# One routing per unit in the sixth layer's experts, each made for the batch that comes next

## The reference, cut to what matters

```python
h = _layernorm(x + attn_out, ln1_g, ln1_b)
flat = h.reshape(-1, C)
probs = jax.nn.softmax(flat @ router_w.T + router_b, axis=-1)
_, top_i = jax.lax.top_k(probs, 2)
assign = jnp.max(top_i, axis=-1)
for e in range(E):                                   # E = 8
    he = jax.nn.gelu(flat @ w1[e].T + b1[e], approximate=False)
    oe = he @ w2[e].T + b2[e]
    out = jnp.where((assign == e)[:, None], oe, out)
return _layernorm(h + moe_out, ln2_g, ln2_b)
```

## Time and profile before

| | us |
|---|---|
| median of 3 runs | 970.46 (965.96 to 972.46) |
| the profiled execution's own time | 972.93 |
| its span, first to last instruction | 970.8 |

### The profile page before, as it was taken

The page is one execution under the profiler, slowest core; times in us unless marked ns, Lnnn a source line. Parts: engine busy times, 40 slices in busy tenths (PEclk is TensorE's granted clock), DMA queues, the critical chain, the costliest instruction groups (busy, mean ns, idle before and its releaser), DMA issues.

```text
span 970.8 us, 13156 instructions
## 1 busy us (share of the span) xinstructions
PE 710.3 (73%) x3874; PEld 463.1 (48%) x3874; DVE 574.3 (59%) x1924; ACT 348.2 (36%) x629; POOL 252.2 (26%) x304
## 2 busy tenths in 40 slices
PE   2677662849919775767875666767888778789998
PEld 1233232838919541223464645456655423346665
DVE  6666654415406361686454355697867766878754
ACT  6355420514505222534432322211323365443321
POOL 2240466350160444323305231141012110100000
PEclk9999865859958775968777875797999999999999
DMA  6273022333524133026212110002244111044440
GB/s 166 58 261 96 28 87 66 115 98 112 141 74 135 52 109 94 20 69 193 80 53 90 47 41 1 0 1 74 89 149 152 49 50 50 2 88 98 90 109 12
DMA packets 76527, 80.08 MB, mean 82 GB/s; under 512 B 9420, under 2 KB 63365, under 8 KB 75178
## 3 DMA queue, kind: packets, MB, share of 16 engines
q1 hardware_dynamic: 58922, 62.59, 22.4%
q0 software_dynamic: 5120, 10.50, 3.7%
q10 hardware_dynamic: 12416, 6.16, 2.2%
HBM read 49.99 MB, written 23.12 MB: 75 GB/s over the span
## 4 chain that ended last, share of the span: by engine, by line
PE 45%; DVE 24%; issue 15%; ACT 6%; another core or an unknown queue 3%; SPq 2%; POOL 2%; DMA 1%; ACTq 1%; DVEq 0%
PE psum_all L951 5%; PE psum_all L967 4%; DVE s_nmx L1385 4%; PE psum_all L748 3%; PE psum_all L724 3%; PE psum_all L726 3%; PE psum_all L863 2%; PE psum_all L850 2%; PE psum_all L852 2%; PE psum_all L705 2%; ACT s_hT L2183 2%; PE psum_all L664 2%; PE psum_all L798 2%; DVE s_stats L1269 2%
## 5 line engine op out<-in xcount | busy, mean ns | idle before, releaser
L2183 ACT ACTIVATE s_hT<-psum_all 77x1024 f32<-77x1024 f32 x96 | 95.8, 1017 | 56.8 <-PE psum_all L726 41.6
L2630 POOL TENSOR_SCALAR s_vare<-s_mv 128x4 f32<-128x4 f32 x40 | 11.3, 281 | 392.4 <-DVE s_mv L1272 383.5
L1385 DVE TENSOR_REDUCE s_nmx<-psum_all 128x4 f32<-128x308 f32 x192 | 83.2, 473 | 47.4 <-PE psum_all L705 45.0
L724 PE MATMUL psum_all<-s_t,s_ks 128*77 128x512 bf16 x192 | 83.6, 436 | 10.8 <-ACT s_hT L2183 7.0
L726 PE MATMUL psum_all<-s_t,s_ks 128*77 128x512 bf16 x192 | 82.9, 432 | 0.0
L705 PE MATMUL psum_all<-s_ks,s_t 128*128 128x308 bf16 x192 | 55.8, 334 | 34.6 <-DVE s_nmx L1385 20.2
L748 PE MATMUL psum_all<-s_hT,s_v 77*32 77x512 f32 x384 | 58.8, 687 | 28.5 <-ACT s_hT L2183 26.6
L2540 POOL DMA_INDIRECT s_w<-routed_y,s_cT x64 | 61.5, 960 | 69.5 <-issue 69.5
L967 PE MATMUL psum_all<-s_arena,s_hT 128*128 x376 | 63.2, 306 | 21.5 <-issue 20.6
L2526 POOL DMA_INDIRECT routed_x<-s_x_normed,s_cT x64 | 62.9, 982 | 50.0 <-DVE s_cT L1605 31.7
L967 PEld LDWEIGHTS psum_all<-s_arena,s_hT 128*128 128x128 f32 x376 | 55.7, 208 | 26.9 <-issue 25.6
(11 more groups left out here) (309 smaller groups left out, 1489.5 us busy)
## 6 DMA issues: line engine op xcount, KB each, us to landing
s_t<-q_parts SPq DMA_DIRECT2D x66, 128.0 KB, 2.9
routed_y<-s_hT ACTq DMA_DIRECT2D x22, 256.0 KB
s_ks<-s_att SPq DMA_DIRECT2D x72, 77.0 KB, 2.1
q_parts<-s_qparts SPq DMA_DIRECT2D x11, 384.0 KB
s_arena<-in_w SPq DMA_DIRECT2D x2, 2048.0 KB, 10.5
s_arena<-choices SPq DMA_DIRECT2D x4, 1024.0 KB, 5.8
s_arena<-gates SPq DMA_DIRECT2D x8, 512.0 KB, 8.0
s_w<-gates SPq DMA_DIRECT2D x8, 512.0 KB, 7.8
```

The lines of the kernel that those rows point to most:

```text
L724: pe.matmul(PS[0:SK, k + y, :], KS1[:, h, keys], T1[:, u % QS, h // HPG, :], start=True, stop=False)
L1385: read(job, dve.tensor_reduce(nmx[:, u % 2, i, HPG * g:HPG * g + HPG], PS[:, k, 0:HPG * SK].rearrange("p (h s) -> p h s", h=HPG), AX.X, AL ...
L2183: read(("S", L, b, p), nc.scalar.activation(Eexp[:, (PAIRS * u + p) % ES, :, :], PS[0:SK, k:k + 2, :], ACT.Exp))
```

## The change

The routing of batch 2 moves from unit 0 (steps 4, 5 and 7) to the first steps of unit 1, and that of batch 3 from unit 1 (steps 0, 3 and 6) to the first steps of unit 2. Unit 0 keeps the routing of batch 1. In SP's list `place_k(2)` moves ahead of `spread_choices(2)`. No instruction is added or removed.

```diff
 MHA_PLACES = {
-    0: [((0, 0, 1), "front", 1), ((1, 1, 1), "R", 1), ((3, 3, 4), "CT", 1),
-        ((4, 0, 5), "front", 2), ((5, 5, 5), "R", 2), ((7, 6, 7), "CT", 2)],
-    1: [((0, 0, 1), "front", 3), ((3, 3, 3), "R", 3), ((6, 6, 6), "CT", 3)],
+    0: [((0, 0, 1), "front", 1), ((1, 1, 1), "R", 1), ((3, 3, 4), "CT", 1)],
+    1: [((0, 0, 0), "front", 2), ((1, 1, 1), "R", 2), ((3, 3, 3), "CT", 2)],
+    2: [((0, 0, 0), "front", 3), ((1, 1, 1), "R", 3), ((3, 3, 3), "CT", 3)],
 }
@@
             spread_choices(1)
+            place_k(2)
             spread_choices(2)
-            place_k(2)
             spread_choices(3)
```

## The result

The changed kernel took 986.07 us (median of 4 runs, 981.33 to 990.90) against 971.46 (4 runs, 965.96 to 972.71). The ratio is 1.0159, interval 1.0118 to 1.0201: slower by some 15 us (14.6 between the medians). I had forecast 989.5 within 980 to 994, +19.0. The time lies well inside the range, but 14.6 is near the low end (+14.0) of what my own terms allowed.

What follows compares the result with a forecast made beforehand. It took units 1 to 3 to be bounded by their first choice multiplies, with SP's queue able to make the rows late. Unit 2 starting 9.9 us later and lasting 9.1 longer gave 970.46 + 19.0 = 989.5 us, range 980 to 994.

Steps and rivals of the forecast that it cites:

- Unit 0, -2.2: Layer 5's experts: unit 0 gets 2.2 us shorter without batch 2's routing, bounds 1.5 and 2.6.
- The third key block 12.95 us into unit 1: Unit 1: copy, routing and choice add 3.0 us, so this block ends 12.95 us after the first multiply, before 9.95.
- SP's block, 22.5 us from its start to the landing: SP's queue: issues to store 16.36 us, to spreading 1.64, landing 4.5; batch 2's rows hold unit 2 until then.
- Unit 2, +9.1: Unit 2 lengthens from 20.5 to 29.6 us: 2.2 copy and clock, 1.9 DVE work, 5.0 new wait; range 6.4 to 10.1.
- The wait ahead of the queries: Unit 2: DVE waits 5.0 us because ACT copies batch 3's turned choice ahead of layer 6's queries; 3.6 at full clock.
- The low clock behind the 12 us wait: Start of unit 2: after 11 us of waiting, PE's first second product and hidden product run slow, costing 1.1 us.
- "Cost nothing" for `place_q(8)`: SP's list before unit 3: place_q(8) follows spread_choices(3), its rows landing at 765.2, 4.6 us before PE wants them.
- The sum, +19.0: Whole program: unit 2 starts 9.9 us later and lasts 9.1 longer, together +19.0 us.
- In time after all: Rival: batch 2's rows arrive in time, only unit 2's own costs stay; total +6, 976.5 us; chance 0.07.
- not slower: Rival: the routing fits the gaps and unit 0's 2.2 us becomes a gain; 968.3 us; chance 0.03.
- The wait, but not unit 2's costs: Rival: unit 2 starts 9.9 us late, but the filled pipeline takes up the routing, 0 to 3 us; 982; chance 0.12.
- Worse by place_q(8): Rival: place_q(8) or batch 3's rows also come late, +3 to +5 us on top; 994 us; chance 0.08.

Runs made afterwards that it cites:

- e1: Changed kernel with spread_choices(2) back ahead of place_k(2) in SP's list, routings left in their new places; ratio 1.0054 to the kernel before.
- e4: Changed kernel with only ACT's copy of batch 3's turned choice in unit 2 at step 4 in place of 3; ratio 1.0197 to the kernel before.
- e5: e3 with the queries' store ahead of the store of batch 3's choice and its spreading in SP's list; ratio 1.0052 to the kernel before.
- e6: e5 with ACT's copies behind the Gelus: turned rows at step 1 in units 1 and 2, turned choice at step 4 in unit 1; ratio 1.0022.
- e7: Changed kernel with 12 of place_k(2)'s 24 issues ahead of spread_choices(2) and 12 behind it; ratio 1.0134 to the kernel before.
- e10: Kernel before with only batch 2's routing moved to unit 1, batch 3's kept there at steps 2, 4, 6, ACT's copies behind the Gelus; ratio 1.0042.
- e2: Kernel before with only SP's two items swapped, place_k(2) ahead of spread_choices(2), routings in their old places; ratio 1.0127.
- e3: e1 with ACT's copy of batch 3's turned choice in unit 2 at step 4 in place of 3, behind the queries; ratio 1.0065 to the kernel before.

## Why the prediction was right, point by point

- **Unit 0, -2.2:** -2.4 (38.3 to 35.9). In e1, e4, e5, e6, e7 and e10 too.
- **The third key block 12.95 us into unit 1:** 12.85 (698.09 to 710.94). The copy ahead of a Gelu holds DVE up by 0.9 us there (1.26 of idle time in place of the 0.33 of the earlier trace rows); I had 1.1, and e6 shows it by taking it away.
- **SP's block, 22.5 us from its start to the landing:** 21.4 (710.94 to 732.35). I took the 16.36 of the earlier trace rows for issues up to the store; it was 15.13, my lower bound of the earlier trace rows. Store to spreading 1.67, landing 4.5 as taken. The 1.2 us are one issue. The block's 24 issues, before and after (shortest, median and longest in ns):

```profile
L2667 SPq DMA_DIRECT2D s_ks<-s_att x24: 524/591/1766, 713.9 to 729.5; - x24
L2667 SPq DMA_DIRECT2D s_ks<-s_att x24: 524/591/592, 710.9 to 725.4; - x24
```

Before, one of the 24 held SP for 1.77 us; after, none took more than 0.59. The other runs have a longest one of 0.59 (e4) to 1.75 (e2), and the whole block 15.1 to 16.6; what holds one issue up is open. Unit 1 +10.9 in place of the +12.0 that follows from my steps. e2 shows the block at work alone, e7 that it is proportional to the issues.
- **Unit 2, +9.1:** +9.65. Its parts: the multiply of expert 2 stands 6.5 us into the unit in place of 3.9, +2.6 (I had 2.2). Against e1, which has the copy but no 12 us wait and its third multiply 4.8 us in, 0.9 of the 2.6 are the copy and 1.7 the low clock (I had 1.1 for each; my own rows 7 gave 1.24 for the clock). The routing on DVE came as costed. The wait ahead of the queries is 3.46, the full-clock value, not the 5.0 that I took for a low clock. I had PE wait some 4 us for multiply 3; it stood 1.73 us and kept its clock. PE in order of time:

```profile
746.51 1.16 PE L813 MATMUL psum_all<-s_w,s_hT 128*128 128x128 f32 x8 [1.73 <-DVE s_hT L1532]
...
754.65 2.08 PE L813 MATMUL psum_all<-s_w,s_hT 128*128 128x128 f32 x8 [3.93 <-DVE s_hT L1532]
```

What I put there came later: the wait for the queries held PE up for 3.93 us at 754.65, and behind it the granted clock was 0.57 (754 to 758) and DVE idle for 3.77 us ahead of the last multiply. So the total is right in part by luck. Up to the multiply of expert 5 the unit is 8.1 us longer and not 9.1, and behind it 1.55 longer, where I had nothing. e1 has the same low clock there (0.50, 666 to 672) without the 12 us wait, so it comes from the order on ACT. e1 against e3, and the change against e4, give the order on ACT 5.1 to 5.3 us of unit 2.
- **The low clock behind the 12 us wait** came as forecast: after 9.82 us without work PE's second product of 733.10 took 2.07 us and the hidden product 1.92, and from 738 on the granted clock was 1.00. Windows of PE, PEld, DVE, ACT and POOL busy (count), granted clock, DMA share, GB/s:

```profile
733.00:738.00 5.00, 4.90 (x19) 3.77 (x20) 2.50 (x11) 0.34 (x1) 1.26 (x2) 0.56 0.23 93
738.00:748.00 10.00, 7.80 (x49) 5.69 (x48) 8.26 (x44) 2.69 (x5) 0.00 (x0) 1.00 0.00 1
754.00:758.00 4.00, 3.35 (x10) 2.54 (x11) 1.20 (x3) 0.00 (x0) 1.89 (x2) 0.57 0.99 326
```

- **"Cost nothing" for `place_q(8)`, with 4.6 us to spare:** right in its cost, wrong in its working. I let the store be waited for as before; it took 7.1 us (752.86 to 759.94) behind the spreading. T1's loads (issued from 759.94, landing 2.5 to 2.8 us after issue) were there some 2 us before PE's first L705 at 765.47. The cover was thinner than I said, and it came from the unit's other delays: e3, e4 and e10, which shorten what stands ahead, lose it.
- **The sum, +19.0:** inside the layer +16.7. The terms that were mis-sized: 1.2 of issue time, and unit 3, which I left as it was and which took 1.4 less (granted clock 1.00 in place of 0.93); unit 2, at +0.55, goes the other way. Between 16.7 and the 14.6 of the medians lie 2.1 us that I put down to scatter in the rest of the program; no run shows it.
- **The rivals.** "In time after all" and "not slower" fell with the 12.06 us. By the figure that the Trainium skill, "DMA: Bandwidth & Descriptors", section "Anatomy of one DMA", gives of GpSimd's path, some 50 ns of dispatch for a DMA, the block would have been 1.2 us long, an estimate. On SP's queue it was 15.1, and 7.5 for half of it; no run here issues these DMAs from GpSimd. "The wait, but not unit 2's costs" fell with 30.2 us, and with e1, whose unit 2 is 28.7 without any wait in front. "Worse by place_q(8)" did not happen here, but is what e3, e4 and e10 show.
- **Left open:** how far PE's clock in unit 3 is chance. It lasts 23.3 to 24.8 us in the seven kernels where no DMA holds it or its start up, with a granted clock of 0.93 to 1.00, and 23.0 and 26.8 in e5 and e6, which start it behind a wait for rows. Timings with intervals of 0.4% to either side cannot part these. And why the timed +0.52% of e5 is not in its trace.

## What to carry to other kernels

A DMA list on one queue is a schedule: before putting a block of many small DMAs ahead of one that someone waits for, multiply its count by the issue time that the trace shows, and compare with the slack of what stands behind. Routing a batch "just in time" for the next unit moves the engines' work without making less of it, and spends the slack of everything that follows it on the way: a store, its wait, a spread load, and each in-order engine's next item. The gain was elsewhere and one number large: a wait of 3.1 us for logits that PE could have made while it stood idle itself, for some 0.4% of the program.

## What the runs showed that I had not expected

- A small store waits for the big loads issued just ahead on the same queue: 16 KB of choices took 5.8 us in place of 1.5 to 2.1 (e2), 384 KB of queries 7.1 to 8.2 in place of 2.3 (after, e4), behind 2 MB of spreading.
- In the experiments the kernel before takes 8.6% less than in the first runs (888 against 971), on both chips that were used. The profiles place the difference ahead of this layer: the first L2028 stands at 580 to 591 us in place of 662 to 666, and behind the layer they agree (the rest is 195.7 to 200.1 in ten kernels, 198.3 in the first two). At one line of the second layer's experts (L951) PE had 16.7 us of idle time before that no shown event ends, and 0.0 in e2. Whether the chip is the cause cannot be said, as the record names none for the first runs; it was not looked for.
